# A selective scan on one Trainium2 core: a pair's sums in two steps, a product with zeros per step, and fewer products on Pool

## The chip, the cores and the metric

The kernel runs on one core of a Trainium2 chip. The metric is the device time of the whole program in microseconds (us). Engine names are those of the profile: PE is the matrix engine (PEld its weight loads), DVE the vector engine, ACT the scalar engine, POOL (here also Pool) the GpSimd engine, SP the engine that issues the transfers.

## The reference

The program is four image layers in a row, each with a selective scan in four directions over two images of 96 channels and 96 x 96 points. What the change touches is the scan, which reads the same in all four layers:

```
def step(hst, inputs):
    ut, dt, bt, ct = inputs
    dA = jnp.exp(dt[..., None] * A)
    hst = hst * dA + (dt * ut)[..., None] * bt[:, :, None, :]
    y = jnp.einsum('bkdn,bkn->bkd', hst, ct)
    return (hst, y)
```

There are 16 states for each of 192 inner channels and each image. Everything around it (projections, convolutions, norms, gates) is left as it is.

## The kernel before

Each layer runs its phases one after the other; `scan` is one phase, so it runs four times. It walks 36 chunks (4 directions of 9) of 1024 points. A chunk is 48 **units**; a unit is 8 channels by 16 states on 128 partitions, by 1024 points. For one unit `u`:

- PE spreads delta and delta times u over the 16 states by a product with a 0/1 matrix (`spread`, line 1667): delta into one of two banks `da`, delta times u into the single bank `p_du`. Each spread is two halves of 512 columns, on other rows of the array: 0 to 63 for delta, 64 to 127 for `p_du`.
- ACT turns `da` into exp(A delta) in place (line 1630), and keeps the last state of a unit (line 1609).
- The product with B, `dbu`, is made by DVE straight from `p_du` (`times_b`, line 1740) for two units of three. For the third, a **shared** unit (`u % 3 == 2`), ACT copies `p_du` to `dus` (line 1604) and Pool multiplies (`share`, line 1562). A share is spread, copied and multiplied three units ahead.
- DVE runs the recurrence (`recur`, line 1753), from `da` and `dbu` to `h`.
- Pool multiplies `h` with C (line 1576) to `hc`.
- PE sums `hc` over the states (`reduce`, line 1684) into one of two banks `p_y`. It does so for a pair of units at once, at every odd unit, nine units late (`SUM_LAG`). After eight units ACT takes the bank out.

The order on each engine is the order of the code; there is no scheduler. DVE's is: product of `u`, recurrence of `u-1`. PE's is, for step `u`: wait for the last product, spread `p_du` (or the next share), at odd `u` the pair's sums, wait for the recurrence of `u-2`, spread `da`. Pool's is: before a unit just ahead of a shared one, the product of the next share; then the C product. The buffers are four `h`, eight `hc`, six `dbu`, two `dus`, so DVE's recurrence can be four units ahead of Pool's C product and no more. Rounds of four chunks (192 units) are written out; the nine rounds are a first, a loop and a last.

Of the kernel before, what the change touches and what calls it, by code (L numbers as in the profile page):

```python
# [13 lines left out]
P = 128  # L14
# [1395 lines left out]
TOTAL = ALL_CHUNKS * UNITS  # L1410
TRIO = 3
DELTA_BANKS = 2
# [5 lines left out]
EIGHT = 8  # L1418
SUM_LAG = 9


# [14 lines left out]
def shared(u):  # L1436

    return u % TRIO == 2

# [6 lines left out]
def scan(nc, l, w, delta_d, du_d, bc_d, y_d):  # L1446
# [6 lines left out]
    with Phase(nc, f"scan{l}") as ph:  # L1453
        T = STEP_T
        H = T // 2
        a_all = ph.sb("a_all", [P, ALL_CHUNKS, UNITS + 1])
        a_dir = ph.sb("a_dir", [P, DIRS, UNITS])
# [46 lines left out]
        with ph.block() as block:  # L1504
# [50 lines left out]
            def _(g):  # L1555
                def share(r, u):
                    g.wait_ge(share_copied, r * (ROUND // TRIO) + (u // TRIO + 1) + ONE)
# [4 lines left out]
                    nc.gpsimd.tensor_tensor(dbu[:, u % DBU_SLOTS, :], bc[:, s, image(u % UNITS), :],  # L1562
                                            dus[:, u // TRIO % DUS_SLOTS, :], ALU.mult).then_inc(share_ready, 1)

                def rounds(r, last):
                    q = r * ROUND
                    for u in range(ROUND):
                        ahead = u + TRIO + 1
                        if shared(ahead) and not (last and ahead >= ROUND):
                            share(r, ahead)  # L1570
                        g.wait_ge(scanned, q + (u + 1) + ONE)
                        if u % PAIR == 0:

                            g.wait_ge(reduced, nth(r * (ROUND // PAIR), (u - HC_SLOTS) // PAIR + 1) + ONE)
                        c = bc[:, slot(u)[0], IMAGES + image(u % UNITS), :]
                        nc.gpsimd.tensor_tensor(hc[:, u % HC_SLOTS, :], c, h[:, u % H_SLOTS, :],  # L1576
                                                ALU.mult).then_inc(hc_ready, 1)
# [3 lines left out]
                g.memset(state[:], 0.0).then_inc(zeroed, 1)  # L1581
                for u in range(TRIO):
                    if shared(u):
                        share(0, u)
                rounds(0, False)
# [5 lines left out]
            def _(a):  # L1591
# [8 lines left out]
                def copy_share(r, u):  # L1600
                    a.wait_ge(share_spread, r * (ROUND // TRIO) + (u // TRIO + 1) + ONE)

                    a.wait_ge(share_ready, nth(r * (ROUND // TRIO), u // TRIO - DUS_SLOTS + 1) + ONE)
                    nc.scalar.activation(dus[:, u // TRIO % DUS_SLOTS, :], p_du[:], ACT.Copy).then_inc(share_copied, 1)  # L1604

# [14 lines left out]
                def rounds(r, first, last):  # L1620
                    q = r * ROUND
                    for u in range(ROUND):
                        if shared(u) and not (last and u + TRIO >= ROUND):
                            copy_share(r, u + TRIO)
                        if u >= DELTA_BANKS or not first:
# [22 lines left out]
                constants_of(0, 0)  # L1648
                a.wait_ge(zeroed, 1 + ONE)
                for u in range(TRIO):  # L1650
                    if shared(u):
                        copy_share(0, u)
                rounds(0, True, False)
# [9 lines left out]
            def _(t):  # L1663
# [9 lines left out]

                def reduce(r, u):
                    n = u // EIGHT
                    if u % EIGHT == 0:

                        t.wait_ge(y_ready, nth(r * (ROUND // EIGHT), n - 1) + ONE)
                    t.wait_ge(hc_ready, r * ROUND + (u + PAIR) + ONE)
                    for half in range(2):  # L1680
                        for v in range(u, u + PAIR):
                            _, j, i = unit(v % UNITS)
                            at = half * 64 + j % 2 * QUAD
                            last = nc.tensor.matmul(p_y[n % 2][at:at + QUAD, :], rsel[:, i, :],  # L1684
                                                    hc[:, v % HC_SLOTS, half * H:(half + 1) * H],
                                                    start=(v % EIGHT < PAIR), stop=(v % EIGHT >= EIGHT - PAIR))
                    last.then_inc(reduced, 1)

                def rounds(r, first, last):
                    q = r * ROUND  # L1690
                    for u in range(ROUND):
                        if u % UNITS == UNITS - 1 and not (last and u == ROUND - 1):

                            s, n = slot(u + TRIO)
                            t.wait_ge(loaded[s], r * (TURNS * LOADS) + n * LOADS + ONE)
                        if first and u == FIRST_UNITS - TRIO:

                            t.wait_ge(loaded[0], LOADS + ONE)

                        t.wait_ge(dbu_ready, r * (ROUND // TRIO * 2) + (u // TRIO * 2 + u % TRIO) + ONE)  # L1700
                        if not shared(u):

                            t.wait_ge(share_copied, r * (ROUND // TRIO) + (u // TRIO + 1) + ONE)
# [11 lines left out]

                t.wait_ge(consts, 48 + ONE)
                t.wait_ge(first_loaded, FIRST_LOADS + ONE)
                for u in range(TRIO):
                    if shared(u):
                        spread_share(0, u)  # L1720
# [3 lines left out]
                rounds(ROUNDS - 1, False, True)  # L1724
                for u in range(ROUND - SUM_LAG + 1, ROUND, PAIR):
                    reduce(ROUNDS - 1, u)

            @block.vector
            def _(d):
                def times_b(r, u, first):  # L1730
                    if first and u == 0:
                        d.wait_ge(first_loaded, FIRST_LOADS + ONE)
                    elif u % UNITS == 0 or first and u == FIRST_UNITS + 1:

                        s, n = slot(u)
                        d.wait_ge(loaded[s], r * (TURNS * LOADS) + n * LOADS + ONE)
                    d.wait_ge(du_spread, r * (ROUND // TRIO * 2) + (u // TRIO * 2 + u % TRIO + 1) + ONE)

# [4 lines left out]
                def recur(r, u):  # L1743
                    v = u % ROUND
                    d.wait_ge(da_ready, r * ROUND + (u + 1) + ONE)
                    if shared(u):
                        d.wait_ge(share_ready, r * (ROUND // TRIO) + (u // TRIO + 1) + ONE)
                    else:
                        d.wait_ge(dbu_ready, r * (ROUND // TRIO * 2) + (u // TRIO * 2 + u % TRIO + 1) + ONE)

# [16 lines left out]

                d.wait_ge(zeroed, 1 + ONE)
                rounds(0, True)
# [1116 lines left out]
```

## Time and profile before

| what | value |
|---|---|
| median of 3 runs | 28189.0 us (28186.71 to 28217.17) |
| the profiled execution | 28208.6 us |
| span of that profile | 28206.8 us |
| share of the span in which DVE, POOL, PE, ACT were busy | 89%, 81%, 81%, 52% |
| granted clock of PE, mean over the span | 0.841 of full speed |

The profile is of one execution. Its page gives each engine's busy time, and a list of groups of instructions by line with their count, busy time, mean duration, and the idle time ahead of them with what ended it. Timelines and tables by stretch come from the same trace. The granted clock is 1.00 at 2.4 GHz and 0.50 at 1.2 GHz; a value between is a mean over a stretch that has both.

### The profile page before, as it was taken

Reading aid. Unit: us, or ns where it says so; the run is one execution under the profiler, and the core shown is the slowest. Engines: PE = TensorE matmul, PEld = TensorE weight load, DVE = VectorE, ACT = ScalarE, POOL = GpSimd, SP = SyncE. Lnnn points to the kernel's source line nnn. Section 1 sums busy time; section 2 is a strip of 40 time slices with the busy share of each in tenths; the row PEclk is TensorE's granted clock in tenths of the full one; section 3 lists DMA queues with packets and bytes.
Section 4 is the critical chain, followed back from the end, with each engine's and each line's share of the span. In section 5 each row is a group of like instructions: output and inputs, shape, how many; then the busy total and the mean of one; then the engine's idle time right before and its main releaser. Section 6 shows DMA issues by size and latency. Waiting matters only on the chain. (4 is left out here: it accounts for less than half of the span.)

```text
span 28206.8 us, 327689 instructions
## 1 busy us (share of the span) xinstructions
PE 22971.4 (81%) x97488; PEld 6672.3 (24%) x97488; DVE 24975.6 (89%) x15875; ACT 14569.4 (52%) x20114; POOL 22942.4 (81%) x10240
## 2 busy tenths in 40 slices
PE   8988888888577888888888888888875888888885
PEld 3322222222232222222233222222212322222222
DVE  2489999999569999999976899999996699999997
ACT  1265555555267555555514555555552655555552
POOL 0179999999047999999971899999980599999992
PEclk9988888888767888888868888888887788888887
DMA  2342222221454221222276312222226622221224
GB/s 87 108 134 49 45 44 49 49 46 36 159 202 155 49 47 42 49 49 46 43 241 227 111 42 49 49 46 43 49 66 215 209 43 46 49 49 41 48 49 147
DMA packets 1121159, 2332.72 MB, mean 83 GB/s; under 512 B 98406, under 2 KB 609346, under 8 KB 1110716
## 3 DMA queue, kind: packets, MB, share of 16 engines
q1 hardware_dynamic: 1117572, 2308.66, 30.1%
q8 instruction: 870, 14.25, 0.2%
q14 instruction: 989, 8.10, 0.1%
q10 hardware_dynamic: 1728, 1.70, 0.0%
HBM read 1329.40 MB, written 980.58 MB: 82 GB/s over the span
## 5 line engine op out<-in xcount | busy, mean ns | idle before, releaser
L1576 POOL TENSOR_TENSOR scan_hc<-scan_bc,scan_h 128x1024 f32<-128x1024 f32 x6912 | 16114.2, 2376 | 125.9 <-DVE scan_h L1753 124.8
L1753 DVE TENSOR_TENSOR_SCAN scan_h<-scan_da,scan_state,scan_dbu 128x1024 f32<-128x1024 f32 x6912 | 15993.9, 2339 | 152.1 <-ACT scan_da L1630 144.1
L1667 PE MATMUL scan_da<-scan_dd,scan_ssel 32*128 32x512 f32 x27648 | 9110.1, 745 | 3004.3 <-DVE scan_h L1753 2769.2
L1630 ACT ACTIVATE scan_da<-scan_da,scan_a_cur 128x1024 f32<-128x1024 f32 x6912 | 7516.4, 1087 | 7740.6 <-PE scan_da L1667 7735.6
L1667 PE MATMUL scan_p_du<-scan_dd,scan_ssel 32*128 32x512 f32 x27648 | 9208.7, 745 | 442.6 <-DVE scan_dbu L1740 171.7
L1740 DVE TENSOR_TENSOR scan_dbu<-scan_p_du,scan_bc 128x1024 f32<-128x1024 f32 x4608 | 5564.6, 1208 | 380.5 <-PE scan_p_du L1667 341.8
L1562 POOL TENSOR_TENSOR scan_dbu<-scan_bc,scan_dus 128x1024 f32<-128x1024 f32 x2304 | 5477.4, 2377 | 61.3 <-ACT scan_dus L1604 59.9
L1667 PEld LDWEIGHTS scan_da<-scan_dd,scan_ssel 32*128 32x128 f32 x27648 | 2452.3, 217 | 10305.3 <-DVE scan_h L1753 8711.5
L1684 PE MATMUL scan_p_y<-scan_hc,scan_rsel 128*32 128x512 f32 x27648 | 4784.9, 773 | 14.9 <-POOL scan_hc L1576 14.4
L1667 PEld LDWEIGHTS scan_p_du<-scan_dd,scan_ssel 32*128 32x128 f32 x27648 | 2415.1, 211 | 3518.3 <-DVE scan_dbu L1740 2945.5
L1609 ACT ACTIVATE scan_state<-scan_h,scan_a_cur 128x1 f32<-128x1 f32 x6912 | 2023.5, 293 | 1580.2 <-DVE scan_h L1753 1469.6
L1604 ACT ACTIVATE scan_dus<-scan_p_du 128x1024 f32<-128x1024 f32 x2304 | 2358.4, 1024 | 148.0 <-PE scan_p_du L1667 101.2
L1041 POOL COPY prep_useq<-prep_grid 128x576 f32<-128x576 f32 (+1 forms) x480 | 606.7, 1316 | 1216.3 <-DMA du_d<-prep_useq 707.8
L1684 PEld LDWEIGHTS scan_p_y<-scan_hc,scan_rsel 128*32 128x32 f32 x27648 | 598.0, 119 | 3219.7 <-issue 2286.0
L1111 DVE SCALAR_TENSOR_TENSOR prep_delta<-prep_p_dt,prep_softplus 128x1152 f32<-128x1152 f32 x288 | 390.9, 1357 | 595.1 <-ACT prep_softplus L1092 574.4
L1051 PE MATMUL prep_p_dbl<-prep_useq,prep_wx 128*128 128x384 f32 x1728 | 772.9, 593 | 104.1 <-DMA prep_wdt<-in_l_wdt 79.5
L781 POOL TENSOR_SCALAR conv_frac<-conv_tanh 36x384 f32<-36x384 f32 x24 | 12.4, 518 | 972.9 <-ACT conv_tanh L872 972.9
L1375 DVE SCALAR_TENSOR_TENSOR prep_useq<-prep_raw,prep_tapv,prep_useq 128x768 f32<-128x768 f32 x432 | 656.0, 1536 | 72.3 <-ACT prep_useq L1326 61.9
L531 POOL MEMSET proj_x<- 32x4608 f32 x1 | 3.9, 3932 | 823.0 <-POOLq L70 823.0
L904 DVE TENSOR_TENSOR conv_top<-conv_diff,conv_p_frac 128x384 f32<-128x384 f32 x72 | 39.9, 554 | 658.6 <-PE conv_p_frac L832 655.7
L1061 PE MATMUL prep_p_dt<-prep_dtv,prep_wdt 13*128 13x384 f32 x1728 | 514.2, 585 | 103.0 <-DVE prep_delta L1111 85.9
L531 POOL MEMSET proj_xn<- 32x1536 f32 x3 | 4.1, 1372 | 666.6 <-POOLq L70 666.6
(222 smaller groups left out, 13255.4 us busy)
## 6 DMA issues: line engine op xcount, KB each, us to landing
scan_bc<-bc_d SPq DMA_DIRECT2D x576, 512.0 KB, 12.0
du_d<-prep_useq SPq DMA_DIRECT2D x384, 576.0 KB, 3.9
delta_d<-prep_delta SPq DMA_DIRECT2D x384, 576.0 KB, 4.4
y_d<-scan_y SPq DMA_DIRECT2D x576, 384.0 KB, 5.2
scan_dd<-delta_d SPq DMA_DIRECT2D x1136, 192.0 KB, 4.8
scan_dd<-du_d SPq DMA_DIRECT2D x1136, 192.0 KB, 6.6
fin_y<-y_d SPq DMA_DIRECT2D x288, 576.0 KB, 5.6
xs_d<-proj_xs_o SPq DMA_DIRECT2D x96, 588.0 KB, 3.3
```

The costliest lines, as they stand in the source:

```text
L1041: g.tensor_copy(dst, src).then_inc(useq_ready, 1)
L1051: last = nc.tensor.matmul(p_dbl[v % 2][:, 0:N], wx[:, chunk(v // PIECES) // CHUNKS, m, :], piece(v)[:, m, :], start=(m == 0), stop=(m == 2))
L1375: nc.vector.scalar_tensor_tensor(out=own, in0=raw[:, m, tap:tap + DW], scalar=tapv[:, m, tap:tap + 1], in1=own, op0=ALU.mult, op1=ALU.add) ...
L1562: nc.gpsimd.tensor_tensor(dbu[:, u % DBU_SLOTS, :], bc[:, s, image(u % UNITS), :], dus[:, u // TRIO % DUS_SLOTS, :], ALU.mult).then_inc(sh ...
L1576: nc.gpsimd.tensor_tensor(hc[:, u % HC_SLOTS, :], c, h[:, u % H_SLOTS, :], ALU.mult).then_inc(hc_ready, 1)
L1604: nc.scalar.activation(dus[:, u // TRIO % DUS_SLOTS, :], p_du[:], ACT.Copy).then_inc(share_copied, 1)
L1609: nc.scalar.activation(state[:, v % UNITS:v % UNITS + 1], h[:, v % H_SLOTS, T - 1:T], ACT.Copy, scale=a_cur[:, s, UNITS:UNITS + 1]).then_i ...
L1630: nc.scalar.activation(da[u % DELTA_BANKS][:], da[u % DELTA_BANKS][:], ACT.Exp, scale=a_cur[:, slot(u)[0], u % UNITS:u % UNITS + 1]).then_ ...
L1667: return nc.tensor.matmul(dst[:, half * H:(half + 1) * H], ssel[rows, i, :], dd[rows, s, m, j, :], start=True, stop=True)
L1684: last = nc.tensor.matmul(p_y[n % 2][at:at + QUAD, :], rsel[:, i, :], hc[:, v % HC_SLOTS, half * H:(half + 1) * H], start=(v % EIGHT < PAI ...
L1740: nc.vector.tensor_tensor(dbu[:, u % DBU_SLOTS, :], p_du[:], bc[:, slot(u)[0], image(u % UNITS), :], ALU.mult).then_inc(dbu_ready, 1)
L1753: nc.vector.tensor_tensor_scan(h[:, v % H_SLOTS, :], da[v % DELTA_BANKS][:], dbu[:, v % DBU_SLOTS, :], state[:, v % UNITS:v % UNITS + 1], ...
```

## The change

Three things change, all in `scan`:

1. **Pool's share.** A table `SHARED` takes the place of `u % 3 == 2`: of each 16 units, 2, 5, 8, 11 and 15 are shared, so Pool makes 15 of 48 products with B and DVE 33, where it was 16 and 32. The counts in the waits are made with `shares(u)` and `products(u)`.
2. **The sums in two steps.** `reduce` gets a `part`. At odd `u` the pair's first 256 columns of each half are summed, at the next, even, step the other 256. The signal `reduced`, which lets Pool use the `hc` buffers again, is given after the second part.
3. **A product with zeros.** Each part also issues one product of `nought` (128 columns of zeros) with all 128 rows of a 0/1 matrix, which adds zeros to 128 columns of the `p_y` bank in use.

The diff, cut to its core:

```
+SHARED = tuple(b + u for b in range(0, UNITS, 16) for u in (2, 5, 8, 11, 15))
+SHARES = UNROLL * len(SHARED)
+PRODUCTS = ROUND - SHARES
+ACTIVE = 128
 def shared(u):
-    return u % TRIO == 2
+    return u % UNITS in SHARED
...
+        nought = ph.sb("nought", [P, ACTIVE])
...
                     for u in range(ROUND):
-                        ahead = u + TRIO + 1
-                        if shared(ahead) and not (last and ahead >= ROUND):
-                            share(r, ahead)
+                        if shared(u + 1):
+                            ahead = next_share(u + 1)
+                            if not (last and ahead >= ROUND):
+                                share(r, ahead)
...
+                def keep_busy(n):
+                    nc.tensor.matmul(p_y[n % 2][:, 0:ACTIVE], ssel[:, 0, :], nought[:], start=False, stop=False)
+
-                def reduce(r, u):
+                def reduce(r, u, part):
                     n = u // EIGHT
+                    cols = slice(part * QUARTER, (part + 1) * QUARTER)
...
+                    opens = u % EIGHT == 0 and part == 0
                     t.wait_ge(hc_ready, r * ROUND + (u + PAIR) + ONE)
+                    if not opens:
+                        keep_busy(n)
...
-                    last.then_inc(reduced, 1)
+                    if part == 1:
+                        last.then_inc(reduced, 1)
+                    if opens:
+                        keep_busy(n)
...
-                        elif not (last and u + TRIO >= ROUND):
-                            spread_share(r, u + TRIO)
-                        if u % PAIR == 1 and (u >= SUM_LAG or not first):
-
-                            reduce(r, u - SUM_LAG)
+                        elif not (last and next_share(u) >= ROUND):
+                            spread_share(r, next_share(u))
+                        if u >= SUM_LAG or not first:
+
+                            if u % PAIR == 1:
+                                reduce(r, u - SUM_LAG, 0)
+                            else:
+                                reduce(r, u - SUM_LAG - 1, 1)
```

On PE, inside a round, two steps of the kernel before (the digits behind `da` and `p_y` number the banks; `x4` or `x2` is a row of that many instructions; each appears as twice as many in the trace):

```order
L1684 MATMUL scan0_p_y1<-scan0_hc,scan0_rsel 32x512 x4
L1667 MATMUL scan0_da1<-scan0_dd,scan0_ssel 128x512 x2
L1667 MATMUL scan0_p_du<-scan0_dd,scan0_ssel 128x512 x2
L1667 MATMUL scan0_da0<-scan0_dd,scan0_ssel 128x512 x2
L1667 MATMUL scan0_p_du<-scan0_dd,scan0_ssel 128x512 x2
L1684 MATMUL scan0_p_y1<-scan0_hc,scan0_rsel 32x512 x4
```

And two steps of the changed kernel at the same kind of place:

```order
L1693 MATMUL scan0_p_y0<-scan0_nought,scan0_ssel 128x128
L1709 MATMUL scan0_p_y0<-scan0_hc,scan0_rsel 32x256 x4
L1685 MATMUL scan0_da1<-scan0_dd,scan0_ssel 128x512 x2
L1685 MATMUL scan0_p_du<-scan0_dd,scan0_ssel 128x512 x2
L1693 MATMUL scan0_p_y0<-scan0_nought,scan0_ssel 128x128
L1709 MATMUL scan0_p_y0<-scan0_hc,scan0_rsel 32x256 x4
L1685 MATMUL scan0_da0<-scan0_dd,scan0_ssel 128x512 x2
L1685 MATMUL scan0_p_du<-scan0_dd,scan0_ssel 128x512 x2
```

Sums now stand in every step, half as wide, with a product of zeros ahead of them, where every second step had no sums.

On Pool, before, a product with B (line 1562) stands between each three products with C:

```order
L1562 TENSOR_TENSOR scan0_dbu<-scan0_bc,scan0_dus 128x1024
L1576 TENSOR_TENSOR scan0_hc<-scan0_bc,scan0_h 128x1024 x3
L1562 TENSOR_TENSOR scan0_dbu<-scan0_bc,scan0_dus 128x1024
L1576 TENSOR_TENSOR scan0_hc<-scan0_bc,scan0_h 128x1024 x3
L1562 TENSOR_TENSOR scan0_dbu<-scan0_bc,scan0_dus 128x1024
```

And in the changed kernel:

```order
L1582 TENSOR_TENSOR scan0_dbu<-scan0_bc,scan0_dus 128x1024
L1597 TENSOR_TENSOR scan0_hc<-scan0_bc,scan0_h 128x1024 x3
L1582 TENSOR_TENSOR scan0_dbu<-scan0_bc,scan0_dus 128x1024
L1597 TENSOR_TENSOR scan0_hc<-scan0_bc,scan0_h 128x1024 x4
L1582 TENSOR_TENSOR scan0_dbu<-scan0_bc,scan0_dus 128x1024
```

Once in 16 units, four C products stand between two B products in place of three.

## Rows read from the trace of the kernel before

**Rows 1.** The page: span, then each engine's busy us, share of span, instructions.

```profile
span 28206.8 us, 327689 instructions
PE 22971.4 (81%) x97488; PEld 6672.3 (24%) x97488; DVE 24975.6 (89%) x15875; ACT 14569.4 (52%) x20114; POOL 22942.4 (81%) x10240
```

**Rows 2.** Table by stretch: first scan and the four's sum; us, engines' busy, clock, DMA.

```profile
1692.70:7040.10 5347.40, 4516.42 (x20716) 1122.68 (x20716) 5230.57 (x2880) 2988.46 (x4279) 5313.95 (x2303) 0.86 0.22 46
...
sum 21383.00, PE 18050.75 PEld 4488.35 DVE 20918.98 ACT 11952.67 POOL 21255.52; mean PE 4512.69 PEld 1122.09 DVE 5229.74 ACT 2988.17 POOL 5313.88
```

**Rows 3.** The page's groups: count, busy us, mean ns, idle ahead and its enders.

```profile
L1576 POOL TENSOR_TENSOR scan_hc<-scan_bc,scan_h 128x1024 f32<-128x1024 f32 x6912 | 16114.2, 2376 | 125.9 <-DVE scan_h L1753 124.8
L1753 DVE TENSOR_TENSOR_SCAN scan_h<-scan_da,scan_state,scan_dbu 128x1024 f32<-128x1024 f32 x6912 | 15993.9, 2339 | 152.1 <-ACT scan_da L1630 144.1
...
L1740 DVE TENSOR_TENSOR scan_dbu<-scan_p_du,scan_bc 128x1024 f32<-128x1024 f32 x4608 | 5564.6, 1208 | 380.5 <-PE scan_p_du L1667 341.8
L1562 POOL TENSOR_TENSOR scan_dbu<-scan_bc,scan_dus 128x1024 f32<-128x1024 f32 x2304 | 5477.4, 2377 | 61.3 <-ACT scan_dus L1604 59.9
L1667 PEld LDWEIGHTS scan_da<-scan_dd,scan_ssel 32*128 32x128 f32 x27648 | 2452.3, 217 | 10305.3 <-DVE scan_h L1753 8711.5
```

**Rows 4.** DVE in order of time at full clock: start us, us, what.

```profile
6020.03 2.34 DVE L1753 TENSOR_TENSOR_SCAN scan_h<-scan_da,scan_state,scan_dbu 128x1024 f32<-128x1024 f32 x1
6022.29 1.20 DVE L1740 TENSOR_TENSOR scan_dbu<-scan_p_du,scan_bc 128x1024 f32<-128x1024 f32 x1
6023.41 4.58 DVE L1753 TENSOR_TENSOR_SCAN scan_h<-scan_da,scan_state,scan_dbu 128x1024 f32<-128x1024 f32 x2
6027.90 1.20 DVE L1740 TENSOR_TENSOR scan_dbu<-scan_p_du,scan_bc 128x1024 f32<-128x1024 f32 x1
6029.02 2.34 DVE L1753 TENSOR_TENSOR_SCAN scan_h<-scan_da,scan_state,scan_dbu 128x1024 f32<-128x1024 f32 x1
```

**Rows 5.** Pool in order of time, the same place.

```profile
6019.82 2.41 POOL L1562 TENSOR_TENSOR scan_dbu<-scan_bc,scan_dus 128x1024 f32<-128x1024 f32 x1
6022.13 7.02 POOL L1576 TENSOR_TENSOR scan_hc<-scan_bc,scan_h 128x1024 f32<-128x1024 f32 x3
6029.05 2.40 POOL L1562 TENSOR_TENSOR scan_dbu<-scan_bc,scan_dus 128x1024 f32<-128x1024 f32 x1
```

**Rows 6.** PE in order of time, ahead of a fall of its clock.

```profile
12018.56 0.70 PE L1667 MATMUL scan_da<-scan_dd,scan_ssel 32*128 32x512 f32 x2 [1.13 <-DVE scan_h L1753]
...
12019.71 1.07 PE L1684 MATMUL scan_p_y<-scan_hc,scan_rsel 128*32 128x512 f32 x8
12020.80 1.13 PE L1667 MATMUL scan_da<-scan_dd,scan_ssel 32*128 32x512 f32 x4
12021.92 1.13 PE L1667 MATMUL scan_p_du<-scan_dd,scan_ssel 32*128 32x512 f32 x4
12024.17 1.13 PE L1667 MATMUL scan_da<-scan_dd,scan_ssel 32*128 32x512 f32 x4 [1.13 <-DVE scan_h L1753]
...
12026.35 1.54 PE L1684 MATMUL scan_p_y<-scan_hc,scan_rsel 128*32 128x512 f32 x8
```

**Rows 7.** Table by stretch, cut where the clock changes; granted clock third from the end.

```profile
12006.33:12026.81 20.48, 16.72 (x86) 4.11 (x84) 20.48 (x12) 13.06 (x19) 20.48 (x10) 1.00 0.00 1
12026.81:12030.22 3.41, 3.41 (x18) 0.95 (x12) 3.14 (x3) 1.25 (x3) 3.41 (x2) 0.50 0.00 0
```

**Rows 8.** The same table for `p_y` alone, ahead of the next fall.

```profile
12033.70:12037.00 3.30, 0.00 (x0) 0.00 (x0) 0.00 (x0) 1.00 0.00 0
```

**Rows 9.** All engines in order of time, inside that stretch at the lower clock.

```profile
12027.82 1.22 PE L1667 MATMUL scan_da<-scan_dd,scan_ssel 32*128 32x512 f32 x2
...
12028.83 1.06 PE L1667 MATMUL scan_da<-scan_dd,scan_ssel 32*128 32x512 f32 x2
...
12030.00 1.23 DVE L1740 TENSOR_TENSOR scan_dbu<-scan_p_du,scan_bc 128x1024 f32<-128x1024 f32 x1 [0.27 <-PE scan_p_du L1667]
```

More of the change, by code:

```diff
@@ L1436, in shared, with shares, products, next_share @@
 def shared(u):
-    return u % TRIO == 2
+    return u % UNITS in SHARED
+def shares(u):
+    return sum(shared(v) for v in range(u))
+def products(u):
+    return u - shares(u)
+def next_share(u):
+    return next(v for v in range(u + 1, u + UNITS) if shared(v))
 def nth(base, n):
@@ L1581, in _ @@
                 g.memset(state[:], 0.0).then_inc(zeroed, 1)
-                for u in range(TRIO):
-                    if shared(u):
-                        share(0, u)
+                g.memset(nought[:], 0.0).then_inc(zeroed, 1)
+                share(0, SHARED[0])
                 rounds(0, False)
@@ L1622, in rounds @@
                     for u in range(ROUND):
-                        if shared(u) and not (last and u + TRIO >= ROUND):
-                            copy_share(r, u + TRIO)
+                        if shared(u) and not (last and next_share(u) >= ROUND):
+                            copy_share(r, next_share(u))
                         if u >= DELTA_BANKS or not first:
@@ L1648, in _ @@
                 constants_of(0, 0)
[L1649 to L1652, printed above, removed]
+                a.wait_ge(zeroed, 2 + ONE)
+                copy_share(0, SHARED[0])
                 rounds(0, True, False)
@@ L1683, in reduce @@
                             at = half * 64 + j % 2 * QUAD
-                            last = nc.tensor.matmul(p_y[n % 2][at:at + QUAD, :], rsel[:, i, :],
-                                                    hc[:, v % HC_SLOTS, half * H:(half + 1) * H],
-                                                    start=(v % EIGHT < PAIR), stop=(v % EIGHT >= EIGHT - PAIR))
-                    last.then_inc(reduced, 1)
+                            last = nc.tensor.matmul(p_y[n % 2][at:at + QUAD, cols], rsel[:, i, :],
+                                                    hc[:, v % HC_SLOTS, half * H + part * QUARTER:half * H + (part + 1) * QUARTER],
+                                                    start=(v % EIGHT < PAIR and part == 0), stop=(v % EIGHT >= EIGHT - PAIR and part == 1))
+                    if part == 1:
+                        last.then_inc(reduced, 1)
+                    if opens:
+                        keep_busy(n)
                 def rounds(r, first, last):
@@ L1716, in _ @@
                 t.wait_ge(consts, 48 + ONE)
+                t.wait_ge(zeroed, 2 + ONE)
                 t.wait_ge(first_loaded, FIRST_LOADS + ONE)
-                for u in range(TRIO):
-                    if shared(u):
-                        spread_share(0, u)
+                spread_share(0, SHARED[0])
                 rounds(0, True, False)
@@ L1724, in _ @@
                 rounds(ROUNDS - 1, False, True)
+                reduce(ROUNDS - 1, ROUND - SUM_LAG - 1, 1)
                 for u in range(ROUND - SUM_LAG + 1, ROUND, PAIR):
-                    reduce(ROUNDS - 1, u)
+                    for part in range(2):
+                        reduce(ROUNDS - 1, u, part)
             @block.vector
@@ L1736, in times_b @@
                         d.wait_ge(loaded[s], r * (TURNS * LOADS) + n * LOADS + ONE)
[L1737 removed]
+                    d.wait_ge(du_spread, r * PRODUCTS + (products(u) + 1) + ONE)
                     d.wait_ge(scanned, nth(r * ROUND, u - DBU_SLOTS + 1) + ONE)
```

28 lines of the change are left out of this document (14 added, 14 removed).

## The prediction

> **What bounds the kernel now.** Start with the page's busy times [rows 1]: DVE 89%, POOL 81%, PE 81%. They are averages over phases with other limits, and the change touches the four scans alone. So the table by stretch comes next [rows 2]. The four scans take 21383 of the 28206.8 us; the other 6824 us are left alone. In the first scan Pool is busy 5314 of 5347 us, DVE 5231, PE 4516. Pool leaves 33 us. Its busy time over its 2303 instructions there is 2.307 us for one. That count is full: 1728 products with C and 576 with B, cut by one at the edge. So **Pool's queue is the scan's length**: 2304 x 2.307 = 5315 us and 33 us of ends and waits.
>
> DVE is close behind. At full clock [rows 4], a product starts 1.12 us ahead of the next recurrence (6022.29 to 6023.41), a recurrence holds DVE 2.26 us, and two in a row 4.49 us, 2.25 each. Three units, with two products, take 8.99 us (6020.03 to 6029.02). Pool needs 9.23 us for the same three (6019.82 to 6029.05) [rows 5]. Per scan, DVE's floor is 1728 x 2.25 + 1152 x 1.12 = 3888 + 1290 = 5178 us, 137 us under Pool. That lead pays for DVE's idle time: 152.1 + 380.5 = 533 us over four scans, 133 per scan, nearly all ended by PE's spread of `p_du` (341.8) or by ACT's exponential of what PE spread (144.1) [rows 3].
>
> Why is PE late? In the scans its granted clock is 0.86 [rows 2]: with s the share of time at 1.2 GHz, 1 - s/2 = 0.86, s = 0.28. Timeline and table show how it falls [rows 6, 7]. PE sums a pair at 12019.71, then for 5.6 us it does spreads alone, with a gap of 1.13 us in which it waits for DVE; the next sums start at 12026.35, and at 12026.81 the clock falls to 0.50. It comes back at 12030.22, after 3.41 us in which PE was busy all the time. The next fall, at 12037.05, stands behind 3.3 us without any sum [rows 8]. During the low stretch a spread pair takes 1.22 + 1.06 us, less overlap, where it took 1.13 us, and DVE waits for `p_du` at 12030.00 [rows 9, 6]. **So the uneven steps of PE (sums in every second one) go with the falls, the falls make PE late, and DVE's lead over Pool pays.**
>
> **The change, part by part.**
>
> *Pool's share.* Per chunk one of 64 Pool instructions goes: per scan 36 x 2.307 = 83 us, over four scans 332 us. Pool's floor becomes 2268 x 2.307 = 5232 us per scan. The 36 products go to DVE: 36 x 1.12 = 40 us, floor 3888 + 1188 x 1.12 = 5219 us. ACT loses 36 copies; Pool waited 59.9 us in all for them [rows 3]. After this both floors are within 13 us, and DVE's cover for PE's lateness falls from 137 us to 13 us. This part alone would give little: DVE's 133 us of idle would lie on the path.
>
> *The sums in two steps.* The same columns are summed in instructions half as wide, so their streaming is the same, and 8 more weight loads per pair come up. The full sums take 1.07 us at full clock [rows 6]; a half lies between 0.53 (all of it scales) and 1.07 (none does). I take 0.63: starts and drain of a group cost once more, some 0.1 us. That is 0.1 us more PE per step, counted over two parts. Now each step of PE holds a `p_du` spread, sums, a `da` spread. One new wait: `reduced` comes a step later, so Pool's C product of an even unit u needs PE's step u+2 in place of u+1. That step's sums stand behind the `p_du` spread, which starts when DVE's product of u+1 ends, 2.25 us before the recurrence of u ends. The spread, zeros and half take 1.13 + 0.5 + 0.6 = 2.2 us: just in time even if Pool had caught up with DVE, and Pool, with the longer floor, mostly lags. Behind that wait stand Pool's next products with C and B, and DVE four units on; I cost it at nothing, up to 0.2 us for an even unit (3456 x 0.2 = 690 us) if PE is late.
>
> *The zeros.* No row shows this product: 128 columns, all rows, in two passes. The nearest is the spread, 1.13 us for two passes of 512 columns (two halves side by side) [rows 6]: a quarter is 0.28 us, the lower end. The upper end is the whole 1.13 us, if it's all fixed cost. In between: a quarter of the streaming and two loads of 0.217 us [rows 3] give 0.28 + 0.43 = 0.71, with the loads counted in part twice. I take 0.5.
>
> PE's budget decides whether that fits. Busy now: 4516/1728 = 2.61 us per step. In the 28% at the lower clock (1497 us per scan) PE was busy all the time, at half speed; at full clock it would save half, 749 us, which leaves 3767/1728 = 2.18 us. With 0.1 + 0.5 it is 2.8 us, in a step that Pool makes 5232/1728 = 3.03 us long. It fits, with 0.2 us left, if the clock stays up.
>
> Does it? Each step now has spreads of both kinds, sums and zeros, 2.8 us of 3.03. The stretches ahead of the falls (spreads alone, and a gap of 1.13 us) don't occur any more: that gap is where the even step's sums and zeros go. I expect the clock in the scans at 0.97 or more.
>
> A rule of the Trainium skill speaks against the zeros: "TensorE: Matmul & The Clock Gate", section "Part 3: Packing small matmuls — row/col tiling", says that weight loads overlap running products only where the row groups differ. The product of zeros takes all four, so its loads and those around it would lie open. Rows 6 agree as far as they go: the spreads of `da` at 12018.56 (0.70 us for a first pass) run beside those of `p_du`, on other rows. By the rule the zeros would be nearer to 0.7 us, the step 3.0 us, and the slower rival below nearer; the sum here goes by the 0.5.
>
> *Sum.* Four scans: -332 us from Pool. Pool's 33 us per scan of ends and waits grow, since the engines run side by side: a tenth of DVE's 133 us, say 12 us per scan, +48. The profiled execution: 28208.6 - 332 + 48 = 27925 us. The median is 19.6 us under it: **27905 us**, -1.0%.
>
> **The rivals.**
>
> *Half of the falls stay.* For: the steps are of uneven length, 3.37 and 2.25 us on DVE, and the loop's ends and the starts of chunks may still thin PE out. Then DVE's floor with half its idle is on the path: 5219 + 67 + 10 (ends) = 5296 us per scan against 5347, -204 us: 27985 us.
>
> *The change doesn't do what it says: the clock falls as before.* For: what the chip counts as activity isn't in the rows; zeros may count little. Against: the sums in every step alone remove the pattern of rows 6. Then 5219 + 133 + 10 = 5362 us, +60 us: 28250 us, about +0.2%; longer low stretches, with more work in them, would make it more.
>
> *PE becomes the bound, and the kernel slower.* The place is between the `p_du` and `da` spreads of each step; the price is the zeros' true cost with the loads that they lay open. At 0.95 us for zeros and split together, PE needs 2.18 + 0.95 = 3.13 us, 5409 us and 33 of ends per scan, 5442: +380 us, 28569 us. It decides from (5347 - 33)/1728 = 3.08 us, that is 0.90 us for the two. Against: PE gains when late, since `da` and `p_du` then run side by side, as at 12018.56.
>
> **How the numbers follow.** The forecast gets 0.67, half of the falls 0.14, falls as before 0.09, PE the bound 0.10. A measurement of this kernel can tell about 0.2% from no change. Faster holds the first two: 0.81. Falls as before is at that border, so 0.07 of it is the same and 0.02, with the last, slower: 0.12. The range takes in the first two with their ends: below, Pool's ends shrinking to 15 us per scan (-72) gives 27785, which needs DVE never late; I stop at 27820. Above, two thirds of the falls give 5219 + 89 + 10 = 5318, 28073; I stop at 28090.
>
> **What the profile after would show.** Right: a scan of about 5275 us; its clock at 0.97 or over; Pool busy to within 45 us, with 2268 instructions; DVE's product at 4752 with idle under 100 us in total; zeros at about 0.25 us per pass; no stretch of 3 us without a `p_y` product. Wrong: a clock still near 0.86; DVE waiting for `p_du` over 300 us; Pool waiting for `p_y` (`reduced`), which it doesn't now; Pool's instruction at other than 2.307 us, since the whole gain is counted in it.

## The result, and the profile after

| | before | changed |
|---|---|---|
| median | 28187.85 us (4 runs) | 27869.49 us (4 runs, 27834.23 to 27884.55) |
| ratio, with its 95% interval | | 0.9885 (0.9873 to 0.9898) |
| span of the profile | 28206.8 us | 27868.2 us |
| the four scans, sum | 21383.0 us | 21074.6 us |

The forecast was 27905 us. The page of the changed kernel begins so (it answers to [rows 1]):

```profile
span 27868.2 us, 410509 instructions
PE 25132.6 (90%) x138960; PEld 9064.9 (33%) x138960; DVE 24949.7 (90%) x16019; ACT 14701.4 (53%) x19970; POOL 22624.7 (81%) x10100
```

The table by stretch, first scan and sum of the four (columns as in [rows 2]):

```profile
1685.60:6950.90 5265.30, 5054.71 (x31028) 1719.50 (x31032) 5221.48 (x2916) 3021.67 (x4243) 5233.65 (x2266) 0.99 0.22 47
...
sum 21074.60, PE 20223.12 PEld 6880.60 DVE 20884.36 ACT 12086.44 POOL 20934.32; mean PE 5055.78 PEld 1720.15 DVE 5221.09 ACT 3021.61 POOL 5233.58
```

The scan went from 5347 to 5265 us, and Pool's busy time from 5314 to 5234: Pool is still the limit, with a shorter queue. The granted clock went from 0.86 to 0.99. The groups (as [rows 3]) show DVE's idle time before the recurrence and the product, 152.1 + 380.5 us before, now 37.5 + 218.4:

```profile
L1597 POOL TENSOR_TENSOR scan_hc<-scan_bc,scan_h 128x1024 f32<-128x1024 f32 x6912 | 16073.0, 2358 | 140.3 <-PE scan_p_y L1709 79.7
L1785 DVE TENSOR_TENSOR_SCAN scan_h<-scan_da,scan_state,scan_dbu 128x1024 f32<-128x1024 f32 x6912 | 15950.5, 2332 | 37.5 <-POOL scan_dbu L1582 28.7
...
L1772 DVE TENSOR_TENSOR scan_dbu<-scan_p_du,scan_bc 128x1024 f32<-128x1024 f32 x4752 | 5684.1, 1196 | 218.4 <-PE scan_p_du L1685 212.0
```

In order of time, inside a scan, PE's new step reads so:

```profile
12002.88 1.13 PE L1685 MATMUL scan_p_du<-scan_dd,scan_ssel 32*128 32x512 f32 x4
...
12003.93 0.49 PE L1693 MATMUL scan_p_y<-scan_nought,scan_ssel 128*128 128x128 f32 x2
...
12004.35 0.64 PE L1709 MATMUL scan_p_y<-scan_hc,scan_rsel 128*32 128x256 f32 x8
...
12005.13 1.13 PE L1685 MATMUL scan_da<-scan_dd,scan_ssel 32*128 32x512 f32 x4
```

The zeros hold PE 0.42 us (12003.93 to 12004.35), the half sums take 0.64 us, and the gap of 1.13 us of [rows 6] has shrunk to some 0.15 us.

Most of the waits that are left stand at the starts of the scans and at the seams between rounds. The same view at one seam:

```profile
5195.32 2.07 PE L1685 MATMUL scan_p_du<-scan_dd,scan_ssel 32*128 32x512 f32 x4 [3.19 <-issue]
...
5197.53 1.22 DVE L1772 TENSOR_TENSOR scan_dbu<-scan_p_du,scan_bc 128x1024 f32<-128x1024 f32 x1 [4.35 <-PE scan_p_du L1685]
...
5199.24 4.65 POOL L1597 TENSOR_TENSOR scan_hc<-scan_bc,scan_h 128x1024 f32<-128x1024 f32 x2 [1.36 <-PE scan_p_y L1709]
```

PE pauses 3.19 us waiting for nothing that the profile shows, its clock falls, DVE waits 4.35 us, Pool 1.36. A scan has eight such seams. Counted over the trace, DVE's 218 us ahead of its product are 66 at the starts of the four scans, 118 at the 32 seams and 34 elsewhere; in the kernel before, 381 us were 69, 97 and 215. What the change took away is the waiting inside the rounds.

### The profile page after: what moved, and what is told of

The parts are those of the page before. It is cut to its first block and busy times, and to the rows that moved or that the text cites. A ratio compares the mean times of both kernels' runs of the same rounds, so it can differ in the third digit from the quotient of the medians.

```text
span 27868.2 us, 410509 instructions
## 1 busy us (share of the span) xinstructions
PE 25132.6 (90%) x138960; PEld 9064.9 (33%) x138960; DVE 24949.7 (90%) x16019; ACT 14701.4 (53%) x19970; POOL 22624.7 (81%) x10100
## 3 DMA queue, kind: packets, MB, share of 16 engines
q10 hardware_dynamic: 1728, 1.70, 0.0%
## 5 line engine op out<-in xcount | busy, mean ns | idle before, releaser
L1597 POOL TENSOR_TENSOR scan_hc<-scan_bc,scan_h 128x1024 f32<-128x1024 f32 x6912 | 16073.0, 2358 | 140.3 <-PE scan_p_y L1709 79.7
L1785 DVE TENSOR_TENSOR_SCAN scan_h<-scan_da,scan_state,scan_dbu 128x1024 f32<-128x1024 f32 x6912 | 15950.5, 2332 | 37.5 <-POOL scan_dbu L1582 28.7
L1685 PE MATMUL scan_da<-scan_dd,scan_ssel 32*128 32x512 f32 x27648 | 7867.9, 645 | 755.4 <-DVE scan_h L1785 39.2
L1685 PE MATMUL scan_p_du<-scan_dd,scan_ssel 32*128 32x512 f32 x27648 | 7905.1, 647 | 210.9 <-DMA scan_bc<-bc_d 109.0
L1772 DVE TENSOR_TENSOR scan_dbu<-scan_p_du,scan_bc 128x1024 f32<-128x1024 f32 x4752 | 5684.1, 1196 | 218.4 <-PE scan_p_du L1685 212.0
L1582 POOL TENSOR_TENSOR scan_dbu<-scan_bc,scan_dus 128x1024 f32<-128x1024 f32 x2160 | 5094.4, 2359 | 56.2 <-ACT scan_dus L1624 56.2
L1709 PE MATMUL scan_p_y<-scan_hc,scan_rsel 128*32 128x256 f32 x55296 | 4444.0, 393 | 0.0
L1693 PEld LDWEIGHTS scan_p_y<-scan_nought,scan_ssel 128*128 128x128 f32 x13824 | 2067.2, 189 | 4976.4 <-issue 3576.6
L1685 PEld LDWEIGHTS scan_p_du<-scan_dd,scan_ssel 32*128 32x128 f32 x27648 | 2115.5, 185 | 4091.8 <-DVE scan_dbu L1772 3812.8
L1693 PE MATMUL scan_p_y<-scan_nought,scan_ssel 128*128 128x128 f32 x13824 | 3392.4, 327 | 1.1 <-POOL scan_hc L1597 1.0
L1685 PEld LDWEIGHTS scan_da<-scan_dd,scan_ssel 32*128 32x128 f32 x27648 | 2084.6, 184 | 3860.1 <-DVE scan_h L1785 3812.8
L1624 ACT ACTIVATE scan_dus<-scan_p_du 128x1024 f32<-128x1024 f32 x2160 | 2210.4, 1023 | 97.7 <-PE scan_p_du L1685 35.2
L1709 PEld LDWEIGHTS scan_p_y<-scan_hc,scan_rsel 128*32 128x32 f32 x55296 | 1091.2, 108 | 1411.1 <-issue 684.2
```

Source lines behind the costliest of these rows:

```text
L1624: nc.scalar.activation(dus[:, shares(u) % DUS_SLOTS, :], p_du[:], ACT.Copy).then_inc(share_copied, 1)
L1685: return nc.tensor.matmul(dst[:, half * H:(half + 1) * H], ssel[rows, i, :], dd[rows, s, m, j, :], start=True, stop=True)
L1693: nc.tensor.matmul(p_y[n % 2][:, 0:ACTIVE], ssel[:, 0, :], nought[:], start=False, stop=False)
L1709: last = nc.tensor.matmul(p_y[n % 2][at:at + QUAD, cols], rsel[:, i, :], hc[:, v % HC_SLOTS, half * H + part * QUARTER:half * H + (part + ...
L1772: nc.vector.tensor_tensor(dbu[:, u % DBU_SLOTS, :], p_du[:], bc[:, slot(u)[0], image(u % UNITS), :], ALU.mult).then_inc(dbu_ready, 1)
L1785: nc.vector.tensor_tensor_scan(h[:, v % H_SLOTS, :], da[v % DELTA_BANKS][:], dbu[:, v % DBU_SLOTS, :], state[:, v % UNITS:v % UNITS + 1], ...
```

## The experiments

The theory: Pool's queue sets the scan; steady PE work keeps the clock up and DVE on time; DVE needs that once its lead is gone. Rivals: the gain is the share alone; it is the clock alone; the zeros are what does it; PE is near its bound. The runs came in three groups, each on one chip with runs of the kernel before beside it (medians 28181 to 28183 us), to which the ratios refer: e1 to e4; e5 and e7 to e9; e10 to e13. "DVE idle" is the sum of the two groups above, over four scans.

| run | sums | zeros | shared of 48 | us | ratio to before (95%) | clock, first scan | DVE idle |
|---|---|---|---|---|---|---|---|
| before | whole | no | 16, every third | 28188 | 1 | 0.86 | 533 |
| changed | two steps | yes | 15 | 27869 | 0.9885 | 0.99 | 256 |
| e1_share16 | two steps | yes | 16, every third | 28198 | 1.0006 (0.9996 to 1.0015) | 0.98 | 606 |
| e2_share15_only | whole | no | 15 | 29234 | 1.0373 (1.0355 to 1.0390) | 0.81 | 1411 |
| e3_split_only | two steps | no | 15 | 27861 | 0.9889 (0.9873 to 0.9906) | 0.99 | 243 |
| e4_zeros_only | whole | yes | 15 | 29798 | 1.0575 (1.0558 to 1.0593) | 0.86 | 1946 |
| e7_uneven16 | whole | no | 16, uneven | 29075 | 1.0318 (1.0301 to 1.0335) | 0.81 | 1385 |
| e8_even15 | whole | no | 15, other places | 28456 | 1.0104 (1.0087 to 1.0121) | 0.85 | 645 |
| e5_zeros256 | two steps | 256 wide | 15 | 27875 | 0.9897 (0.9880 to 0.9913) | 0.99 | 266 |
| e9_split_lag7 | two steps, lag 7 | no | 15 | 27851 | 0.9887 (0.9870 to 0.9903) | 0.99 | 242 |
| e11_gap_even | whole | no | 15, 12 for 11 | 28648 | 1.0163 (1.0140 to 1.0186) | 0.84 | 812 |
| e12_zeros_share16 | whole | yes | 16, every third | 30120 | 1.0685 (1.0667 to 1.0703) | 0.84 | 2503 |
| e13_split_share14 | two steps | no | 14 | 28012 | 0.9936 (0.9919 to 0.9952) | 0.99 | 225 |
| e10_split_unroll12 | two steps | no | 15 | 27802 | 0.9863 (0.9847 to 0.9880) | 0.99 | 162 |

### One part at a time

**Share back to 16, the rest kept.**

```
-SHARED = tuple(b + u for b in range(0, UNITS, 16) for u in (2, 5, 8, 11, 15))
+SHARED = tuple(range(2, UNITS, 3))
```

> The changed kernel with Pool's share put back to 16 of 48 (u % 3 == 2); sums in two steps and zeros stay. Theory (Pool's queue sets the scan; steady PE work only keeps DVE on time): the scans' granted clock is 0.97 or more, DVE's idle before lines 1785 and 1772 falls from 533 us to under 250, and yet the time stays at 28170 to 28200 us, since Pool still has 2304 instructions of 2.307 us per scan. Rival (the higher clock itself is worth time, by whatever path): 28000 us or less. Rival (the gain is the share alone and the clock plays no part): also about 28190, so this run tells only the second rival apart.

Measured 28198 us, no change that can be told, at a clock of 0.98. The high clock by itself is worth nothing while Pool has 2304 instructions per scan. DVE's idle was expected to fall to under 250 us; it is 606, and its group says why.

```profile
L1785 DVE TENSOR_TENSOR_SCAN scan_h<-scan_da,scan_state,scan_dbu 128x1024 f32<-128x1024 f32 x6912 | 15978.0, 2340 | 371.0 <-POOL scan_hc L1597 230.4
```

DVE now waits 230 us for Pool's C product, which it never did long in the kernel before, and 124 us for Pool's product with B: with PE on time, DVE runs into the limit of four units. The lead is there, and unused.

**The share alone.** `reduce` is that of the kernel before, called at odd steps only, and `keep_busy` is gone; `SHARED` is that of the changed kernel.

> The kernel before with only Pool's share changed to 15 of 48: a pair's sums whole at odd steps, no product of zeros. Theory: the clock in the scans stays near 0.86, DVE keeps its 533 us of idle or more, now without a lead over Pool: 5219 + 133 + 10 = 5362 us per scan, 28200 us, range 28080 to 28260. Rival (the gain is the share alone): Pool stays the limit and the time is that of the changed kernel, 27870 us.

Measured **29234 us, +3.7%**, far outside both. Pool, which was to be the limit, sits idle for 1494 us:

```profile
L1597 POOL TENSOR_TENSOR scan_hc<-scan_bc,scan_h 128x1024 f32<-128x1024 f32 x6912 | 16135.0, 2350 | 1494.3 <-DVE scan_h L1775 1481.2
...
L1762 DVE TENSOR_TENSOR scan_dbu<-scan_p_du,scan_bc 128x1024 f32<-128x1024 f32 x4752 | 5743.2, 1209 | 1195.1 <-PE scan_p_du L1685 1160.4
```

So "the gain is the share alone" has fallen, and something costs 267 us per scan more than the theory's 5362. The next sections look for it.

**Without the zeros.**

```
-                    if not opens:
-                        keep_busy(n)
...
-                    if opens:
-                        keep_busy(n)
```

> The changed kernel without the products of zeros: 15 of 48, sums in two steps. If sums in every step are what keeps the clock up: clock in the scans 0.97 or more and 27850 to 27880 us, a little under the changed kernel if anything. If the zeros are needed too: clock between 0.86 and 0.95, DVE idle of 250 us or more, 27950 to 28150 us.

27861 us and 0.99, first branch. The zeros are not needed. (The split does two things at once: it puts sums in every step, and it makes twice as many instructions of half the width. Whole sums of one unit in each step weren't run, so which of the two keeps the clock up isn't told apart.) The first scan has PE busy 4352 of 5265 us, 83%, less than the kernel before had (84%), and the clock holds:

```profile
1679.10:6943.80 5264.70, 4351.99 (x27612) 1214.80 (x27616) 5220.55 (x2916) 3022.12 (x4243) 5232.11 (x2267) 0.99 0.22 47
```

**Zeros without the split.** The sums are whole at odd steps; the even step has a product of zeros, which gives the signal `reduced`.

```
+                def close(u):
+                    keep_busy(u // EIGHT, u % EIGHT == EIGHT - PAIR).then_inc(reduced, 1)
```

> The changed kernel with the sums whole at odd steps again, but zeros in every step (15 of 48; the signal that frees the hc buffers comes with the even step's zeros, as late as in the changed kernel). If zeros suffice whatever the spread of the sums: clock 0.97 or more, 27860 to 27900 us. If sums have to stand in every step: clock 0.86 to 0.95 and 27950 to 28200 us. With the zeros' 0.42 us ahead of whole sums of 0.87 us in odd steps, a da spread may start up to 0.2 us late, which its slack of about 1 us covers.

29798 us at 0.86: with whole sums, zeros don't hold the clock up. The clock is above the 0.81 of the share alone, and the time is still 564 us worse, and far above the range of its second branch, too.

**The zeros twice as wide**, `ACTIVE = 256`.

> The changed kernel with zeros of 256 columns in place of 128. A product of zeros takes 0.42 us in its trace; twice the columns should take about 0.63. Theory (PE has room, and gains when late, since da and p_du spreads then run side by side): 27860 to 27960 us, clock in the scans 0.99, DVE idle for p_du somewhat over 212 us. Rival (PE near its bound: busy 2.92 us of each 3.05 us step in the changed kernel, 3.13 with this): 5409 us per scan and ends, 28500 us.

27875 us, as the theory had it. PE is busy 5235 of 5266 us, and the others hardly wait for it more than before (DVE for `p_du` 214 us in place of 212, Pool for `p_y` 97 in place of 80):

```profile
1694.90:6961.00 5266.10, 5235.39 (x31034) 1716.93 (x31034) 5221.28 (x2916) 3023.66 (x4243) 5236.06 (x2266) 0.99 0.22 47
```

In order of time, inside a scan:

```profile
12001.75 1.13 PE L1685 MATMUL scan_da<-scan_dd,scan_ssel 32*128 32x512 f32 x4
12002.76 1.13 PE L1685 MATMUL scan_p_du<-scan_dd,scan_ssel 32*128 32x512 f32 x4
12003.82 0.70 PE L1693 MATMUL scan_p_y<-scan_nought,scan_ssel 128*128 128x256 f32 x2
12004.45 0.64 PE L1709 MATMUL scan_p_y<-scan_hc,scan_rsel 128*32 128x256 f32 x8
```

The zeros hold PE 0.63 us where it was 0.42, as expected. But PE's busy time rose by 0.10 us per step and not by 0.21, to 3.03: spreads that are late follow each other closer (here 1.01 us from start to start; it was 1.12). So the rival's 3.13 us per step didn't come about, and the rival has fallen at this width. At which width PE does become the bound wasn't measured.

### Why the share alone costs 3.7%: count or places?

In the share-alone kernel the stretches between changes of the clock (columns as in [rows 7]) are no longer scattered:

```profile
12041.14:12047.97 6.83, 6.83 (x26) 1.90 (x24) 5.21 (x4) 2.67 (x4) 6.02 (x3) 0.50 0.00 0
12047.97:12054.80 6.83, 5.19 (x26) 1.17 (x24) 6.81 (x5) 3.42 (x6) 5.24 (x4) 1.00 0.00 1
12054.80:12061.62 6.82, 6.82 (x26) 1.96 (x28) 5.45 (x3) 2.46 (x4) 5.87 (x3) 0.50 0.00 0
12061.62:12068.45 6.83, 5.35 (x28) 1.21 (x22) 6.57 (x4) 4.82 (x7) 5.78 (x3) 1.00 0.00 0
```

And inside the third, PE and DVE in order of time:

```profile
12055.66 4.58 DVE L1775 TENSOR_TENSOR_SCAN scan_h<-scan_da,scan_state,scan_dbu 128x1024 f32<-128x1024 f32 x2
12055.80 2.08 PE L1685 MATMUL scan_p_du<-scan_dd,scan_ssel 32*128 32x512 f32 x4
...
12057.81 1.94 PE L1706 MATMUL scan_p_y<-scan_hc,scan_rsel 128*32 128x512 f32 x8
...
12059.68 1.22 PE L1685 MATMUL scan_da<-scan_dd,scan_ssel 32*128 32x512 f32 x2
12059.69 1.22 PE L1685 MATMUL scan_p_du<-scan_dd,scan_ssel 32*128 32x512 f32 x2
...
12061.86 1.23 DVE L1762 TENSOR_TENSOR scan_dbu<-scan_p_du,scan_bc 128x1024 f32<-128x1024 f32 x1 [1.61 <-PE scan_p_du L1685]
```

This is unit 15 of its 16, shared and odd; the product at the end is that of the next unit. At a shared unit DVE has two recurrences in a row, 4.5 us. In that time PE must spread the next share, and then `p_du` for DVE. At an odd unit the whole sums stand between. At the lower clock the row takes 2.0 + 1.9 + 2.2 us, from 12055.80 to 12061.86 with the hand-over, and DVE loses 1.61 us. At an even shared unit the sums are missing and the row would take 2.0 + 2.2 us: it fits. At full clock both fit. The count over whole traces at the end of this section bears that out.

Is it the places, then, and not the count?

```
+SHARED = (2, 5, 8, 11, 15, 18, 21, 24, 27, 31, 34, 37, 40, 42, 45, 47)
```

> Whole sums at odd steps, no zeros, Pool's share 16 of 48 as in the kernel before, but at uneven places: 2 5 8 11 15 18 21 24 27 31 34 37 40 42 45 47. Pool's and DVE's floors are those of the kernel before (5315 and 5178 us per scan). Theory A (the count: with 15 of 48 DVE lost its lead, and that is why the share alone took 29234 us): 28150 to 28250 us. Theory B (the places: uneven gaps between shared units make PE's steps thin out in step with the clock's falls, and PE and DVE lose time in low stretches whatever Pool does): over 28500 us, the clock in the scans under 0.84, Pool idle over 200 us.

29075 us: with the very counts of the kernel before, and whole sums, uneven places cost 3.2%. Theory B: the loss comes although DVE has its lead over Pool.

```
+SHARED = (2, 6, 10, 14, *range(17, UNITS, 3))
```

> Whole sums at odd steps, no zeros, share 15 of 48, with the three gaps of four units together: 2 6 10 14, then every third unit from 17 to 47. Theory A (count): as with the other fifteen, 29150 to 29300 us. Theory B (places): nearer to the kernel before, since 33 of 48 units have its gaps: 28200 to 28700 us, with a clock in the scans of 0.83 to 0.86.

28456 us, clock 0.85: B again. With 15 shared and the gaps of four ending at even units the loss is 1.0%. This 1.0% is mostly the part of the count: DVE's idle, 645 us, is only 112 us more than in the kernel before, but with the lead gone it lies on the path, and the kernel is 268 us slower.

```
+SHARED = tuple(b + u for b in range(0, UNITS, 16) for u in (2, 5, 8, 12, 15))
```

> As the kernel with the share alone (whole sums at odd steps, no zeros, 15 of 48), but with the gap of four ahead of unit 12 in place of 15: shared are 2 5 8 12 15 of each 16. Theory: the 1.6 us that DVE loses once in 16 units come where a gap of four ends at an odd shared unit at the lower clock: PE then has the share's spread (2.1), whole sums (1.9) and the next spreads (2.3) in a row, 6.2 us, against DVE's two recurrences, 4.5 us. At an even shared unit the sums are missing from that row, 4.4 us, and nothing is lost. So most of the loss goes: 28250 to 28600 us, and the low stretches still come ahead of unit 12. Rival (any gap of four costs this, wherever it ends): 29100 to 29300 us.

28648 us. One number in the table, 12 for 11 in each 16 units, takes back 586 of the 1046 us. It ends just above the range: unit 15 is still shared and odd, and some low stretches still meet it. (The "once in 16 units" above is too simple: in the first of the four stretches shown for the share-alone kernel, unit 11 costs DVE 1.61 us as well, at 12047.66.)

**The same row, with zeros in it.** The even-gapped kernel before, with zeros in every step, as in the zeros-only kernel but with `SHARED = tuple(range(2, UNITS, 3))`. As there, `reduced` comes with the even step's zeros, one step later than in the kernel before; Pool waits 88 us for it in all, so that this is not what costs the time:

> The kernel before (whole sums at odd steps, every third unit shared) with zeros of 128 columns in every step. It shows what zeros do to the clock where nothing else is changed. Theory (what holds the clock up is the sums in every step, zeros add little): clock in the scans stays at 0.84 to 0.90, and since each low stretch then has more work in it, 28200 to 28500 us. Rival (zeros hold the clock up where the gaps between shared units are even): 0.97 or more and 28170 to 28200 us.

The clock (0.84) is as the theory had it; the time, **30120 us, +6.9%**, is not. Cut where the clock changes:

```profile
12015.96:12029.61 13.65, 12.23 (x66) 4.29 (x62) 13.36 (x8) 7.74 (x11) 11.69 (x6) 1.00 0.22 54
12029.61:12036.44 6.83, 6.83 (x24) 1.73 (x22) 4.81 (x3) 2.29 (x3) 6.83 (x4) 0.50 0.01 2
12036.44:12050.09 13.65, 12.23 (x66) 4.29 (x62) 13.35 (x8) 8.38 (x13) 11.70 (x6) 1.00 0.00 1
12050.09:12056.92 6.83, 6.83 (x24) 1.72 (x22) 4.83 (x3) 2.29 (x3) 6.83 (x4) 0.50 0.01 2
```

In this window the pattern repeats exactly, and in the first scan 242 of 271 low stretches last 6.83 us: 20.48 us, which is six units, the period of "every third shared, every second summed". Each low stretch meets the same place, the odd shared unit:

```profile
12029.84 4.58 DVE L1785 TENSOR_TENSOR_SCAN scan_h<-scan_da,scan_state,scan_dbu 128x1024 f32<-128x1024 f32 x2
12029.98 2.07 PE L1685 MATMUL scan_p_du<-scan_dd,scan_ssel 32*128 32x512 f32 x4
...
12031.99 0.79 PE L1693 MATMUL scan_p_y<-scan_nought,scan_ssel 128*128 128x128 f32 x2
...
12032.71 1.94 PE L1708 MATMUL scan_p_y<-scan_hc,scan_rsel 128*32 128x512 f32 x8
...
12036.72 1.22 DVE L1772 TENSOR_TENSOR scan_dbu<-scan_p_du,scan_bc 128x1024 f32<-128x1024 f32 x1 [2.29 <-PE scan_p_du L1685]
```

In six units DVE has 18.2 us of work and loses 2.29 us, which gives the 20.48. PE was busy 12.23 of the 13.65 us ahead of the fall, 90%.

**The whole traces.** The table counts, in the four scans, the shared units whose next product DVE reached with PE at the lower clock (for over half of the 5 us ahead of it), and DVE's idle time ahead of these products.

| run | odd shared units, met at the lower clock | DVE idle there, us | even shared units, met | DVE idle there, us |
|---|---|---|---|---|
| before | 210 of 1148 | 168 | 243 of 1152 | 19 |
| e2_share15_only | 799 of 1292 | 951 | 368 of 864 | 28 |
| e7_uneven16 | 576 of 1292 | 745 | 271 of 1008 | 64 |
| e8_even15 | 147 of 860 | 156 | 231 of 1296 | 28 |
| e11_gap_even | 280 of 860 | 350 | 236 of 1296 | 28 |
| e4_zeros_only | 914 of 1292 | 1653 | 11 of 864 | 10 |
| e12_zeros_share16 | 1031 of 1148 | 2310 | 12 of 1152 | 12 |

At full clock DVE loses some 30 us at most behind the odd ones in any of these kernels. So the price is the number of meetings times 0.8 to 1.3 us, or 1.8 to 2.2 us with zeros in the row.

### Is 15 the right share, and what is left?

With `SHARED = (2, 5, 8, 12, 15, 19, 22, 26, 29, 33, 36, 40, 43, 47)`:

> The changed kernel without zeros and with 14 of 48 shared (2 5 8 12 15 19 22 26 29 33 36 40 43 47). With the clock up DVE's floor is the limit: 1728 x 2.25 + 1224 x 1.12 = 5259 us per scan, 5285 to 5305 with ends, against 5265 with 15 of 48: 27950 to 28030 us, Pool idle 95 us per scan or more. Rival (places matter here too, as they do with whole sums): over 28100 us.

28012 us, where the sum of DVE's instructions puts it, with Pool idle for 554 us before its C products. With the clock up, this uneven table shows no cost of its places, and floors made of counts times durations hold. Of 14, 15 and 16 shared, 15 is the balance.

The wait for the sums, with `SUM_LAG = 7` and no zeros:

> The changed kernel without zeros and with the sums seven units late in place of nine, so that Pool has its hc buffers back two steps sooner. Theory (Pool's wait for the sums, 80 us in all in the changed kernel, stands at the ends of rounds and is a real loss): Pool's idle ended by p_y gone, 27790 to 27850 us. Rival (that wait only takes the place of a wait for DVE at the same spot): 27850 to 27875 us, as with the split alone.

27851 us, on the border of the two ranges; the profile decides for the rival. Pool's idle before its C product stays at 131 us and is merely ended by DVE now.

```profile
L1597 POOL TENSOR_TENSOR scan_hc<-scan_bc,scan_h 128x1024 f32<-128x1024 f32 x6912 | 16065.2, 2355 | 131.3 <-DVE scan_h L1781 131.2
```

Fewer seams, with `UNROLL = 12` and no zeros:

> The changed kernel without zeros, with rounds of 12 chunks written out in place of 4, so that each scan has 3 rounds and not 9. In the changed kernel the few stretches at the lower clock, and most of Pool's idle (some 2 us each), stand at the 8 seams between rounds, where PE pauses for 2.6 to 3.3 us. Theory (the seams cost Pool 2 us each): 6 fewer per scan, 24 in all, 27790 to 27830 us. Rival (longer code brings as many pauses of its own, for its instructions): 27850 us or more.

**27802 us**, the fastest of all, 1.4% under the kernel before. By the times alone it is hardly apart from the split with nine rounds (the intervals of the two ratios overlap); by the profiles it is: a scan takes 5247 us in place of 5265, and Pool's idle before its C product is 61.6 us in place of 131.5:

```profile
1693.10:6940.10 5247.00, 4351.64 (x27600) 1220.09 (x27604) 5223.23 (x2916) 3022.09 (x4243) 5231.60 (x2266) 0.99 0.22 47
```

## Why the prediction was right, and where it wasn't

The time (27905 against 27869 us) and the path were right; one step was badly wrong, in a place that the changed kernel doesn't visit. That the two times lie within 36 us is in part luck: the profiled execution was forecast at 27925 us and took 27870, with 24 us of the difference in the scans and 30 outside them, and the allowance of 19.6 us from profile to median, of which the changed kernel's runs show 0.5, took some of it back.

- **What bounds the kernel: right.** Pool's queue. The run with the share put back shows it most plainly: clock up, no time gained, DVE waiting for Pool.
- **Pool's term: right.** Forecast -332 us; the four scans' Pool busy time fell by 321, at 2.31 us per instruction as before.
- **The +48 us for waits side by side: over-sized.** Pool's idle and ends per scan were to grow from 33 to 45 us. Over the four scans they went from 127 to 140 us in all, 32 to 35 per scan: +13 and not +48. The lateness of PE inside the rounds is gone (215 us of DVE's idle, now 34), and what is left are the starts and the seams, which both kernels have. The scans fell by 308 us, against a forecast of 284. The rest of the difference of the two profiles, 30 us, lies outside the scans, where the code is the same; among the profiles here that part ran from 6729 to 6833 us.
- **The clock: right in size, and in half of the cause.** 0.97 or more was forecast, 0.99 came. The prediction gave it to sums and zeros together, 2.8 us of work in each step. The split does it without the zeros (0.99 with 2.52 us of work), and whole sums with zeros don't (0.86 and 0.84).
- **Zeros at 0.5 us, halves at 0.63: right** (0.42 and 0.64). PE's busy time per step came to 5055/1728 = 2.93 us against 2.8. The term that was too small is the one under them: without zeros PE needs 4352/1728 = 2.52 us, where the prediction had 2.18 + 0.1. It took the low stretches as the same work at half speed. But there the spreads of `da` and `p_du` run side by side, two in 2.1 us (12027.82 to 12029.90 in the kernel before), and at full clock one after the other, 1.13 us each, two take longer than that. This explanation is read from the rows; no run tests it. The gain that I gave the zeros a part in is not theirs: without them the time is the same (27861 us).
- **"This part alone would give little": wrong.** The step that failed is the size of DVE's idle time in "DVE's 133 us of idle would lie on the path", and with it the price of the rival "falls as before", 28250 us. That the idle lies on the path was right: with 15 shared it does, in e2 (5219 + 353 = 5572 of 5629 us per scan) and in e8 (5219 + 161 = 5380 of 5426). But the share alone takes 29234 us, since its idle is 353 us per scan and not 133. DVE's idle isn't a constant of the kernel that one may carry over: it hangs on which step of PE the low stretches meet. In the kernel before they met 210 of 1148 odd shared units; with the new table of shared units they met 799 of 1292. The prediction looked at how much DVE has to do, and not at what stands in PE's row between two of DVE's products.
- **"PE becomes the bound": the wrong mechanism for a real danger.** I looked for it in PE's total per step, 3.08 us. Zeros twice as wide took PE's busy time to 99% of the scan, 3.03 us per step, and cost nothing; its 3.08 us were never reached. The slower kernels are slower by one row, at the lower clock alone, with PE's total far from the limit in e2 (4830 of 5629 us). The zeros do lengthen that row, by 0.7 us at the lower clock.
- **What the profile after would show: two signs missed.** DVE's idle ahead of its product was to be under 100 us and is 218; the starts and seams alone make 184. And Pool waits for `p_y` (`reduced`), 79.7 us, which was named as a sign of being wrong. It costs nothing here: with the sums seven units late that wait is gone, Pool is idle as long, and the time is the same (27851 us, without zeros; 27861 with lag nine).
- **The loads of the zeros.** The Trainium skill, "TensorE: Matmul & The Clock Gate", section "Part 3: Packing small matmuls — row/col tiling", has weight loads overlap running products only where the row groups differ, and the prediction put the zeros nearer to 0.7 us by it. The trace agrees as far as it goes, in that the loads of the zeros start at 12003.93 with their product and not ahead of it. But all of it takes 0.42 us, and there is no loss on the path at either width.

What stays open is what a product of zeros does to the clock. Where sums were whole, adding it took the mean from 0.81 to 0.86 with 15 shared and from 0.86 to 0.84 with 16, and in neither kept it up; whether its data or its width is the reason, no run shows. Open too is why the low stretches lock to the pattern of one kernel and drift over that of another; the runs show that they do, and where the locking falls decides the price.

## What to carry to other kernels

Before a change of balance between two engines, look at the third that feeds both: lay out its row between two hand-overs, at either clock level, and compare it with the time that the consumer gives it. Where work comes in every second step, spreading it over all steps shortens the longest row and, here, also kept the clock up; work made up to keep an engine busy did neither. Idle time that is measured under one order of the work isn't a constant to be carried into another. And before the slack between two engines is spent, ask what it was paying for.

## What the runs showed of the hardware that I had not expected

- **Busy share doesn't tell whether the clock stays up.** It held at 0.99 with PE busy 83% of the scan (split, no zeros) and fell again and again with 93% (5427 of 5844 us, clock 0.84: whole sums with zeros in every step). Nor does the longest pause of PE: in that kernel only 20 of its waits in the four scans were longer than 1 us, while the clock fell 271 times in the first scan alone.

```profile
1678.30:7522.60 5844.30, 5427.45 (x24144) 1726.16 (x24145) 5229.87 (x2880) 2991.69 (x4279) 5334.52 (x2303) 0.84 0.20 42
```

- **The falls can lock to the loop.** In that kernel 6.83 us low and 13.65 us high repeat in step with six units, so that nearly each fall meets the same instructions and the loss is at its worst, 2.29 us.
- **One entry in a table of places** (12 for 11, in each 16 units) moved the time by 2%, with every count the same.
- **The seams of written-out rounds** cost some 3 us each: with 24 fewer the four scans took 73 us less (21059 to 20987 us), and the program 60 (27861 to 27802 us).
